# Router, second norm and first expert weights moved into the output projection; the last sum of each attention core moved forward; expert gates two steps behind

## What is computed

```python
x = x + tanh(g_xattn[n]) * xattn_n(layernorm(x), ctx)
x = x + tanh(g_ffn[n]) * ffn_n(layernorm(x))
```

```python
h = rmsnorm(x, rms_weight)                 # layer 3 only
probs = softmax(h @ router_w); topv, topi = top_k(probs, K)
y = sum_e w[:, e] * (silu(h @ w_gate[e]) * (h @ w_up[e])) @ w_down[e]
```

## Time and profile before

| | us |
|---|---|
| median of 3 runs (2488.28 to 2488.78) | 2488.33 |
| the profiled execution, its own time | 2486.28 |
| its span in the trace | 2484.5 |
| PE busy in the span | 2277.2 (92%) |
| DVE, POOL, ACT busy | 1557.1, 1431.8, 1043.9 |
| mean granted TensorE clock, share of full | 0.935 |

### The profile page before, as it was taken

The page is one execution under the profiler, slowest core; times in us unless marked ns, Lnnn a source line. Parts: engine busy times, 40 slices in busy tenths (PEclk is TensorE's granted clock), DMA queues, the critical chain, the costliest instruction groups (busy, mean ns, idle before and its releaser), DMA issues. The chain is left out here.

```text
span 2484.5 us, 31100 instructions
## 1 busy us (share of the span) xinstructions
PE 2277.2 (92%) x11508; PEld 1580.0 (64%) x11508; DVE 1557.1 (63%) x2538; ACT 1043.9 (42%) x1522; POOL 1431.8 (58%) x870
## 2 busy tenths in 40 slices
PE   6889999899999976698999999879997999999878
PEld 5677887766666652565566666467886566666567
DVE  4566653377878757765787887442224787878432
ACT  3434443355555524211455555323332555554332
POOL 0442200188888872266688888734442788888733
PEclk9889998799999986698899999879998999999879
DMA  1025563111111013001111111022211111110010
GB/s 34 20 76 157 180 193 98 50 38 57 38 56 38 26 51 112 29 1 38 38 38 52 43 38 44 1 73 83 83 33 51 38 38 56 38 56 26 1 54 22
DMA packets 49842, 136.48 MB, mean 55 GB/s; under 512 B 7469, under 2 KB 13437, under 8 KB 49244
## 3 DMA queue, kind: packets, MB, share of 16 engines
q1 hardware_dynamic: 49308, 134.16, 17.6%
q10 hardware_dynamic: 384, 0.33, 0.1%
HBM read 121.26 MB, written 13.21 MB: 54 GB/s over the span
## 5 line engine op out<-in xcount | busy, mean ns | idle before, releaser
L2139 DVE TENSOR_REDUCE mx<-psum 128x1 f32<-128x500 f32 x1008 | 652.4, 675 | 231.9 <-PE psum L1232 219.6
L1662 ACT ACTIVATE E<-psum 125x896 f32<-125x896 f32 x576 | 528.2, 920 | 586.7 <-PE psum L1253 559.3
L1906 POOL TENSOR_TENSOR SA<-SA,E 125x896 f32<-125x896 f32 x288 | 609.7, 2117 | 22.6
L1261 PE MATMUL psum<-E,V 125*64 125x448 f32 x2304 | 471.7, 545 | 0.0
L1232 PE MATMUL psum<-K,Q 128*128 128x500 f32 x1008 | 358.9, 411 | 20.8 <-ACT Q L1649 11.2
L1251 PE MATMUL psum<-Q,K 128*125 128x448 f32 x1152 | 331.7, 369 | 2.3 <-ACT E L1662 2.3
L1253 PE MATMUL psum<-Q,K 128*125 128x448 f32 x1152 | 329.8, 367 | 0.0
L1261 PEld LDWEIGHTS psum<-E,V 125*64 125x64 f32 x2304 | 152.9, 136 | 231.0 <-issue 223.4
L1232 PEld LDWEIGHTS psum<-K,Q 128*128 128x128 f32 x1008 | 189.0, 191 | 166.0 <-issue 45.4
L1906 POOL TENSOR_TENSOR SA<-SA,SB 125x896 f32<-125x896 f32 x96 | 200.3, 2086 | 157.8 <-DVE SB L2160 157.8
L1251 PEld LDWEIGHTS psum<-Q,K 128*125 128x125 f32 x1152 | 213.0, 187 | 36.7 <-ACT E L1662 6.9
(11 more groups left out here) (294 smaller groups left out, 3731.9 us busy)
## 6 DMA issues: line engine op xcount, KB each, us to landing
K<-kt_scratch SPq DMA_DIRECT2D x48, 750.0 KB, 4.9
K<-kt_scratch SPq DMA_DIRECT2D x48, 375.0 KB, 6.0
EW<-in_f_w SPq DMA_DIRECT2D x64, 256.0 KB, 6.6
kt_scratch<-kt SPq DMA_DIRECT2D x16, 750.0 KB, 4.3
WS<-in_f_w SPq DMA_DIRECT2D x31, 384.0 KB, 4.7
WoT<-in_a_WoT SPq DMA_DIRECT2D x24, 256.0 KB, 2.6
V<-in_ctx SPq DMA_DIRECT2D x16, 375.0 KB
Wq<-in_a_Wq SPq DMA_DIRECT2D x16, 256.0 KB, 3.1
```

What stands on the lines that cost most here:

```text
L1261: i = e.matmul(psum[c * DC:(c + 1) * DC, 4 + b % 2, 0:HT], V[0:LP, b, k * DC:(k + 1) * DC], E[g[n, b, k] % NE][0:LP, half[c]], start=k == ...
L1662: e.activation(E[m % NE][0:LP, :].rearrange("p (c q) -> p c q", c=2), psum[0:LP, pair:pair + 2, 0:HT], ACT.Exp).then_inc(exp_set.sem, 1)
L1906: e.tensor_tensor(SA[b % 2][0:LP, :], a[0:LP, :], x[0:LP, :], ALU.add).then_inc(sum_set.sem, 1)
L2139: e.tensor_reduce(mx[:, b % 2, j * 3 + c:j * 3 + c + 1], psum[:, bank, 0:CW], AX.X, ALU.max).then_inc(small_free.sem, 1)
```

## The change

1. Last batch of each core: POOL adds only up to block 7; `total` moves up, between the values blocks 7 and 8, and multiplies four tiles (SA, the second pair sum SB, E of blocks 10 and 11) with the ones. CH and CL of tile 0 are made at the core's end, ahead of the barrier (layers 1 to 3).
2. Projection, all layers: PSUM banks 0 to 2 in place of 0 to 3; in layers 0, 2 and 3, CL of the odd tiles is made on DVE (tile 3 of layer 3 stays on POOL).
3. Layers 2 and 3: the loads of the router matrix, the RMS weights and the first four weight blocks are issued at the start of the projection. The first two splits, the RMS norm tile by tile, the transposition (2 tiles behind in layer 2, 4 in layer 3) and the router products (one tile behind that, into bank 3) run within it.
4. Experts of layers 2 and 3: `gate` two steps behind `up`, `down` four; the router in three parts (softmax before the first `up`, top-k after slot 0's, transposition and copy after slot 2's); side tasks from step 2.
5. Memory is laid out anew for this.

The diff, cut to its core:

```diff
+LAST_ADDED = 7
+TURN_BEHIND = {0: 2, 1: 0, 2: 2, 3: 4}
+TURNED_NORM = {0: 1, 2: 5, 3: 8}
...
     for k in range(len(slots) + 4):
         if k < len(slots):
             n, c = slots[k]
-            if c == 0 and n + 3 < blocks:
+            if c == 0 and 4 <= n + 3 < blocks:
                 order.append(("fetch", n + 3))
             order.append(("up", n, c))
+        if k in (0, 2):
+            order.append(("route", 1 + k // 2))
+        for x in {2: (), 3: (0, 1)}.get(k, (k - 2,)):
+            if 0 <= x < len(slots):
+                order.append(("gate", *slots[x]))
+        if k >= 4:
+            order.append(("down", *slots[k - 4]))
...
                     order.append(("add", b, 9))
+                    order += [("total", b)] if b == B - 1 else []
...
-    order += [("values", B - 1, NL - 1)]
-    return order + [("total", B - 1), ("div", B - 1)]
+    return order + [("values", B - 1, NL - 1), ("div", B - 1)]
...
+    def by_pool(b, k):
+        return k in ADDED and (b < B - 1 or k <= LAST_ADDED)
+    def low_by_pool(n, i):
+        return n == 1 or i % 2 == 0 or (n, i) == (3, 3)
...
+                terms = [SA[b % 2]]
+                if b < B - 1:
+                    e.wait_ge(*sum_set.at(n, b, NL - 1))
+                else:
+                    e.wait_ge(*sum_set.at(n, b, LAST_ADDED))
+                    e.wait_ge(*pair_set.at(n, b, 9))
+                    e.wait_ge(*exp_set.at(n, b, NL - 1))
+                    terms += [SB[1], E[g[n, b, 10] % NE], E[g[n, b, 11] % NE]]
...
     def pe_project(e, n):
+        behind = TURN_BEHIND[n]
+        for i in range(NT + behind + 1 if behind else NT):
+            if i < NT:
+                e.wait_ge(*low_flag(n, i).at(n, i))
+                if i >= 3:
+                    e.wait_ge(*x_out.at(n, i - 3))
...
+            if behind and 0 <= i - behind < NT:
+                pe_project_turn(e, n, i - behind)
+            if n in (2, 3) and i > behind:
+                pe_logits(e, n, i - behind - 1)
...
     def act_project(e, n):
+        act_part(e, n, 1)
+        for i in range(NT + behind if behind else NT):
             if i + 2 < NT:
+                act_part(e, n, i + 2)
+            if n != 1 and i in (4, 5):
+                act_split(e, n, i - 4)
+            if n == 3 and 0 <= i - 1 < NT:
+                act_square(e, i - 1)
+            if behind and i >= behind:
+                act_project_turn(e, n, i - behind)
...
     def pool_project(e, n):
         for i in tiles:
+            if i + 2 < NT and low_by_pool(n, i + 2):
+                low_part(e, n, i + 2)
             pool_rstd(e, 1 + 2 * n, i)
+            if n != 1 and i in (5, 6):
+                pool_split(e, n, i - 5)
+            if n == 3 and i >= 2:
+                pool_rms(e, i - 2)
...
     def dve_project(e, n):
+        if not low_by_pool(n, 1):
+            low_part(e, n, 1)
+        for i in range(NT + behind + 1 if behind else NT):
+            if i + 2 < NT and not low_by_pool(n, i + 2):
+                low_part(e, n, i + 2)
+            if n != 3 and behind and 0 <= i - behind < NT:
+                dve_turn(e, r, i - behind, 4 + (i - behind) % 4)
...
+            if n == 3:
+                dve_rms(e, i)
```

More of the change, by code:

```diff
@@ L164, in context_order, with expert_order @@
     return steps + [[("cstore", B - 1)]]
-def expert_order(blocks, free, routing, side, last):
+def expert_order(blocks, side):
     slots = [(n, c) for n in range(blocks) for c in range(2)]
-    order = [("fetch", n) for n in range(3)] + [("split", 0), ("split", 1)]
-    routing, side = [("route", s) for s in range(routing)], list(side)
-    for k in range(len(slots) + 3):
+    order = [("fetch", n) for n in range(4)] + [("split", 0), ("split", 1), ("route", 0)]
+    side = list(side)
+    for k in range(len(slots) + 4):
         if k < len(slots):
             n, c = slots[k]
-            if c == 0 and n + 3 < blocks:
+            if c == 0 and 4 <= n + 3 < blocks:
                 order.append(("fetch", n + 3))
             order.append(("up", n, c))
-        if 0 <= k - 1 < len(slots):
-            if slots[k - 1] == (free, 0):
-                order += routing
-                routing = []
-            order.append(("gate", *slots[k - 1]))
-        if k >= 3:
-            order.append(("down", *slots[k - 3]))
-            if slots[k - 3] == (blocks - 1, 0):
+        if k in (0, 2):
[5 more added lines that the diff above has]
+            order.append(("down", *slots[k - 4]))
+            if slots[k - 4] == (blocks - 1, 0):
                 order += [t for step in side for t in step]
@@ L190, in expert_order @@
         if k < len(slots):
-            if k < 2 * free:
-                order += routing[:1]
-                routing = routing[1:]
-            elif side:
+            if side and k >= 2:
                 order += side.pop(0)
@@ L382, in upper_uses @@
             out.append(("ynorm", t[1]))
-        elif t[0] == "route" and t[1] == (7 if f == 0 else 1):
+        elif t[0] == "route" and t[1] == (7 if f == 0 else 2):
             out += [("turn_gates", a) for a in range(2)]
@@ L504, in build @@
     at(top)
-    CH = [mem.take("CH", [P, H // 2, P], F32R) for _ in range(3)]
-    CL = [mem.take("CL", [P, H // 2, P], F32R) for _ in range(3)]
+    CH = [mem.take("CH", [P, H // 2, P], F32R)]
+    at(top + (4 * L + 31) // 32 * 32)
+    CH.insert(0, mem.take("CH", [P, H // 2, P], F32R))
+    CL = [mem.take("CL", [P, H // 2, P], F32R)]
+    assert mem.at <= after_k1
+    CH.append(mem.take("CH", [P, H // 2, P], F32R))
+    CL += [mem.take("CL", [P, H // 2, P], F32R) for _ in range(2)]
     parts_end = mem.at
@@ L632, in build @@
             m[name] = [mem.take(name, [P, 768], d) for _ in range(4)]
-        here = mem.at
         at(w_at)
@@ L638, in build @@
         assert mem.at <= norm_end
-        at(here)
-        for name, d in (("HF", F32), ("HH", F32R), ("HL", F32R)):
-            m[name] = [mem.take(name, [P, HT], d) for _ in range(4)]
-        top_n = TOP2 if f == 2 else TOP3
+        at(base)
+        wide = E2 * I2 if f == 2 else E3
+        m["selr"] = mem.take("selr", [64, wide], F32R)
+        m["HF"] = [mem.take("HF", [P, HT], F32) for _ in range(4)]
+        high_at = mem.at
+        m["HH"], m["HL"] = ([mem.take(n, [P, HT], F32R) for _ in range(4)] for n in ("HH", "HL"))
+        high_end = mem.at
+        at(high_at if f == 2 else high_end)
+        m["sel"] = mem.take("sel", [64, wide], F32)
+        assert f == 3 or mem.at <= high_end
+        at(max(high_end, mem.at))
         m["lmax"], m["lexp"] = mem.take("lmax", [P, NT], F32), mem.take("lexp", [P, NT, n_exp], F32)
@@ L1295, in pe_project_turn, with pe_logits @@
         pe_turn(e, r, i, 4 + i % 4)
+    def pe_logits(e, f, i):
+        m, n_exp = ffn[f], {2: E2, 3: E3}[f]
+        if i == 0:
+            e.wait_ge(*gate_w_set.at(f))
+        e.wait_ge(*yl_set.at(TURNED_NORM[f], i))
+        pairs = []
+        for kd in range(KD):
+            pairs += split_pairs(YH[:, kd, tok(i)], YL[:, kd, tok(i)], m["GH"][:, kd, :], m["GL"][:, kd, :])
+        t = product(e, psum[:, 3, i * n_exp:(i + 1) * n_exp], pairs)
+        if i == NT - 1:
+            t.then_inc(logits_made.sem, 1)
     def pe_experts(e, f):
@@ L1426, in pe_experts @@
                 p.then_inc(pos_made.sem, 1)
-            elif kind == "route" and t[0] == (7 if f == 0 else 1):
+            elif kind == "route" and t[0] == (7 if f == 0 else 2):
                 for a, group in enumerate((range(0, 4), range(4, NT))):
@@ L1704, in act_experts @@
         m, free, swiglu = ffn[f], FFN_FREE[f], SWIGLU[f]
-        if f == 3:
-            for i in tiles:
-                e.wait_ge(*y_set.at(7, i))
-                if i > 0:
-                    e.wait_ge(*act_own.now())
-                t = e.activation(m["sq"][:, :], Y[:, i, :], ACT.Square, accum_out=m["ss"][:, i:i + 1])
-                t.then_inc(*(act_own.up() if i < NT - 1 else (sq_set.sem, 1)))
-            for i in tiles:
-                act_turn(e, 8, i, 4 + i % 4)
         for kind, *t in FFN[f]:
             if kind == "split":
-                if f != 0 or t[0] >= 2:
+                if t[0] >= 2:
                     act_split(e, f, t[0])
@@ L1888, in pool_core @@
                 lows = (n, b, 5)
-            elif kind == "scores" and t[0] in ADDED:
+            elif kind == "scores" and by_pool(b, t[0]):
                 k = t[0]
@@ L2201, in dve_project @@
     def dve_project(e, n):
[L2202 to L2211 removed]
+        r, behind = 1 + 2 * n, TURN_BEHIND[n]
```

213 lines of the change are left out of this document (100 added, 113 removed).

## The result

The kernel after takes **2444.82 us** (median of 4 runs, 2443.06 to 2447.68) beside 2488.31 for the kernel before: a ratio of 0.9826 (95% interval 0.9809 to 0.9843). It is 43.5 us faster, where I had forecast 60; the range ended at 2442. The direction was right, the time lies 2.8 outside.

What follows compares the result with a forecast made beforehand. PE was busy 92% of the span, the rest lost to idling or low clock behind chains through other engines. Terms 8.3+27.8+25.6 = 61.7, less 1.7, gave 60 off 2486.3, 2426.3; plus 2.05 for the median, 2428 (range 2418 to 2442).

Steps and rivals of the forecast that it cites:

- Layer 1 and the cores' ends: Layer 1's projection: DVE's queue starts 8.3 us earlier; core ends shorter by 3.8 (layer 1) and 4.5 (layers 2, 3).
- The rival by which they get no shorter: Cores' ends: the total waits for the pair sum, the whole 4.5+4.5+3.8 is lost, 2441 us; chance 0.07.
- Layer 2, 27.8: Layer 2's projection and experts: first down comparably reached at 1646.0 instead of 1673.84, a gain of 27.8 us.
- the 0.4 of the router matrix cost nothing: Layer 2's projection: loads, splits and the router matrix's 0.4 us add no time.
- the 4.0 from X to the last YL: Layer 2's projection tail: YL of tile 6 is there 4.0 us after DVE takes up the last tile.
- Layer 3, 25.6: Layer 3's projection and experts: first down comparably at 2385.5 instead of 2411.14, a gain of 25.6 us.
- the last tile is done at 24.9: Layer 3's projection: queue waits delay the last tile from 21.0 to 24.9 us after the barrier.
- YL needs power, scaling and ACT's turn: Layer 3's projection: tile 6 stands 2.4 us behind the first router product, which waits for this YL.
- The slow starts: Expert starts of layers 2 and 3: clock below full for 4 to 6 us, costing 2.6 each.
- clock kept: Rival: the granted clock stays up over the projection tails, both slow starts go, 2421 us; chance 0.13.
- Ports: Rival: low parts on DVE take 1.5 us more each beside POOL, up to 12 us, 2440 us; chance 0.16.
- Steady steps, tail, slower: Expert steps stay 4.2 us, tail gains 0; slower rival: ring of four hidden tiles adds 75 us, 2503; chance 0.03.

Runs made afterwards that it cites:

- e7: Kernel after with the total back at the cores' end with one term and POOL adding all blocks: 2459.8 us, ratio 0.9866 to 0.9896.
- e1: Kernel after with layer 2's router matrix split in DVE's step 1 of the projection instead of step 3: 2436.6 us.
- e4: Kernel after, nothing moved, with 116 idle matmuls on PE ahead of products where it waited in the projections of layers 2 and 3: 2433.3 us.
- e6: e5 plus idle matmuls on PE in the projection tails (26 in layer 2, 50 in layer 3): 2426.5 us.
- e12: Kernel after with 14 idle matmuls on PE in the opening of layer 3's core: 2438.6 us.
- e3: Kernel after with ACT's squares in layer 3's projection made one step later: 2440.3 us.
- e2: Kernel after with DVE making YL of tile k-5 ahead of X of tile k in layer 3: 2437.7 us.
- e9: Kernel after with CL of all tiles of layers 2 and 3 made on POOL again: 2442.9 us, ratio 0.9795 to 0.9846.
- e10: e5 with layer 3's two weight splits moved to the end of POOL's stage: 2427.0 us.
- e5: Kernel after with early router-matrix split in layer 2 and, in layer 3, YL ahead of X and squares one step later: 2428.4 us.

## Why the prediction was wrong

**Layer 1 and the cores' ends: right**, in term and mechanism (8.3 against 8.2; 3.7, 4.8 and 4.5 for the cores; e7 takes it back). The rival by which they get no shorter is out.

**Layer 2, 27.8 against 20.9.** The step that failed is "the 0.4 of the router matrix cost nothing". I had priced its two instructions on DVE, but not asked when the first router product would want them. They stand behind X, statistics and Y of tile 3, and PE reaches that product with tile 3's last matmul: 2.83 of wait. This lets the clock fall for tile 4. e1 took 4.6 of the projection's miss of 7.1 back with one moved step (and lost 1.8 again in the experts). Of the 2.5 that are left, the tail from X of tile 6 has 0.9 from the clock (7.33 against 6.47 in e4 and e6), for I had costed its router products at the full clock; the rest is mostly Y of tile 6, 1.1 late behind YL of tile 5 in DVE's loop (1621.18 and 1621.52 above), where the old code had them the other way round, and then 0.4 longer than usual beside a split of POOL. I took the 4.0 from X to the last YL out of the old trace; it became 5.7. This last point is read, not tried.

**Opening of layer 3, 0 against -3.2.** I had no term for this. What took 2.8 of it is a fall of the clock in the core's opening (see e12). Whether the change brings it on or chance does stays open.

**Layer 3, 25.6 against 16.2.** The step that failed is "the last tile is done at 24.9": it was 30.9. I followed the four queues at the full clock throughout. At that clock (e4) it is 27.1, and e4's whole projection is 5.8 shorter, so more than half of the miss of 9.4 is clock. Of the queues I had the squares holding CH, but their result (DVE's wait for CH of tile 5, with X of tile 3 behind it) came sooner and cost 4.0 (e3), with the stretched Y in it. And of the router product I wrote that its "YL needs power, scaling and ACT's turn", leaving out what matters: YL stands at the end of DVE's step, behind X of the tile that PE has only just finished. Each of the first two router products waits for that by construction, 2.43 and 2.22; e2 gave 7.0 back. Tail: 9.9 forecast, about 13 measured, 2.0 of it clock (11.05 in e4).

**The slow starts** of the experts came as I had them (5 and 4 us), and so did the first downs. I treated the clock as a matter of the starts only and gave "clock kept" 0.13; the case that came, a clock that falls within the projections, I had not among the rivals. In the kernel before, the clock was down for the first 8.0 and 7.5 us of these two projections, behind the core's end, and again in their tails; between these the clock was 1.00 (1610.4 to 1634, 2347.5 to 2368), and PE went through its tiles without a wait. The change took the first away and put waits and falls into the middle.

**Ports**, my rival, had the right kind of cost in the wrong place. The low parts on DVE took 1.23 each. But Y, with a single tensor operand, was stretched beside POOL. Timeline of layer 3, POOL and DVE:

```profile
2327.21 2.38 POOL L1721 TENSOR_TENSOR CL<-QR,CH 128x1024 fp32r<-128x1024 f32 x1 [0.62 <-ACT CH L1716]
2327.57 2.17 DVE L2075 TENSOR_SCALAR Y<-X,mv,rstd 128x256 f32<-128x256 f32 x1
...
2342.42 1.81 POOL L1991 TENSOR_TENSOR WL<-WS,WH 128x768 fp32r<-128x768 f32 x1
2342.75 1.63 DVE L2075 TENSOR_SCALAR Y<-X,mv,rstd 128x256 f32<-128x256 f32 x1
```

Y usually takes 0.40; these two and the one of 1.64 end 0.15 after POOL's instruction, 4.2 more in all, and layer 2's last Y (0.80) ends 0.16 after one. In e9, with more low parts on POOL, a scaling took 2.61 instead of 0.48 besides. e10 gained 1.2 in its tail where it moved such a POOL instruction away. How much of the kernel's miss these stretches are, no run shows by itself: the one of 1.64 stands in the chain of e3, the one of 2.17 has slack behind it (DVE next waits 0.80 for PE), and that of 1.63 stands ahead of PE's fourth wait.

**Steady steps, tail, slower:** no fourth-tile wait; layer 2's experts keep PE busy for all of 190 us in a row, and from the first output copy of ACT to the end it is 6.4 in both kernels.

Together, 6.9 in layer 2, 9.4 in layer 3 and 3.2 in the opening between them are the 19.5 that the account lacks.

## What to carry to other kernels

When work moves into a stage that another engine bounds, follow each small product back to its place in the producer's queue, not to its duration: a tile that the consumer wants "one step behind" must be made ahead of the producer's own wait in that step. Price a wait on PE in the middle of dense work at its length and about half as much to three quarters again (1.3 behind 2.83 in layer 2, 5.8 behind 8.1 in layer 3), for the clock can fall behind it; and prefer moving the producer over filling the wait (three moves gave 16, fillers 11 alone and 2 on top). Where a gap decides on the clock, traces of equal code differ by a few us: compare stages, and more than one trace, before a difference is called chance or an effect.

## What the runs showed of the hardware

- The clock falls in the middle of full work, after the wait is over: PE waited until 1604.44 and the matmuls slow down from 1606.7; it came back near 1610. In layer 3 the second fall lasted through a whole tile, 2333.6 to 2340.4.
- The same instructions and gaps do or don't bring a fall, as shown for the opening of layer 3 (14.0 or 11.2) and for the gates of layer 2 (e5 against the kernel after). The Trainium skill (TensorE: Matmul & The Clock Gate, What's actually happening) says that what watches the engine's activity runs freely of the program, so that one kernel starts up differently from run to run. These traces agree only in part: they are one each of different kernels, and the fall at the gates came with the early split in four of four and without it in none of seven, which is hardly chance.
- A one-operand DVE instruction from SBUF to SBUF stood until POOL's tensor_tensor beside it was over: 0.40 became 1.63 to 2.17. I had quoted half of the rule: the Trainium skill (GPSIMD Engine Reference, Specifications) names, beside instructions with two SBUF inputs, those in a two-port mode, and by another page of the Trainium skill (VectorE: DVE Perf Modes, What auto-detection actually checks) the engine takes such a mode where a single source and the destination are in SBUF and their outermost dimensions are even or equal. These rows agree in that the instruction waits; the mode itself no trace shows.
